# A graph kernel's last stage: VectorE's waits on its own signals become drains, fewer signals per group, another order of its step

## The reference, cut to what matters

```python
h = x @ W
e = jax.nn.leaky_relu((h @ a1)[src] + (h @ a2)[dst], negative_slope=0.2)
attention = jax.nn.softmax(e)                      # over all edges
msgs = attention[:, None] * h[src]
x = _layernorm(x + jax.ops.segment_sum(msgs, dst, num_segments=N))
```

## Time and profile before

| what | us |
|---|---|
| median of three runs | 1265.93 |
| lowest and highest of them | 1257.95, 1266.73 |
| the profiled execution, its own time | 1259.13 |
| its span | 1257.4 |

### The profile page before, as it was taken

How to read it: one execution, slowest core, us unless ns; L and a number is a source line. 1 busy time by engine, 2 the same in 40 slices (tenths; PEclk the granted TensorE clock), 3 DMA queues, 4 the chain that set the end, 5 groups by cost and what they waited for, 6 DMA issues and landing times.

```text
span 1257.4 us, 14313 instructions
## 1 busy us (share of the span) xinstructions
PE 718.7 (57%) x3271; PEld 482.5 (38%) x3271; DVE 759.0 (60%) x3537; ACT 717.2 (57%) x2048; POOL 764.1 (61%) x807
## 2 busy tenths in 40 slices
PE   0357767767667767676844564546455554544441
PEld 0235445445445544444634454545442211111110
DVE  4487767767777668677756555546437444444442
ACT  3457777777777777777713343424347554444443
POOL 7665666666666666665056665666654666666666
PEclk9888888787887888878967777767767766777775
DMA  7365565566665656654155767667755333433331
GB/s 211 110 187 158 184 209 168 178 188 214 203 200 200 203 161 193 197 166 163 68 171 162 216 207 221 198 211 223 208 172 163 121 113 115 119 116 120 107 107 46
DMA packets 89104, 209.87 MB, mean 167 GB/s; under 512 B 20602, under 2 KB 22793, under 8 KB 89008
## 3 DMA queue, kind: packets, MB, share of 16 engines
q1 hardware_dynamic: 63802, 161.20, 40.4%
q0 software_dynamic: 25216, 47.76, 13.6%
HBM read 122.85 MB, written 90.07 MB: 169 GB/s over the span
## 4 chain that ended last, share of the span: by engine, by line
another core or an unknown queue 19%; DVE 17%; ACT 13%; issue 8%; PE 5%; POOL 1%; DMA 1%; DVEq 0%; SPq 0%; POOLq 0%
ACT yb L801 3%; ACT node_out L801 2%; ACT src_b L952 2%; PE psum L748 2%; DVE src_b L1477 2%; DVE match L1152 2%; ACT xsT L961 2%; DVE nst L1492 1%; DVE nst L1254 1%; POOL out_dram L524 1%; DMA x1d_in<-x_all 1%; DVE shift L1485 1%; ACT h_res L965 1%; DVE node_in L1247 1%
## 5 line engine op out<-in xcount | busy, mean ns | idle before, releaser
L518 POOL DMA_INDIRECT xs<-in_x,src_tab x196 | 185.7, 947 | 153.0 <-remote 74.6
L524 POOL DMA_INDIRECT out_dram<-yb,at_last x196 | 194.7, 993 | 120.7 <-ACT yb L801 64.6
L518 POOL DMA_INDIRECT xs<-x_all,row_tab x196 | 187.5, 957 | 114.9 <-issue 55.8
L518 POOL DMA_INDIRECT h_res<-in_x,dst_tab x196 | 188.9, 964 | 59.8 <-issue 59.8
L801 ACT ACTIVATE h_res<-node_in,shift,rstd 128x128 f32<-128x128 f32 (+1 forms) x392 | 155.8, 482 | 0.3 <-DVE shift L1284 0.3
L776 PE MATMUL psum<-src_b,ident_inv 128*128 128x512 f32 x90 | 69.6, 865 | 132.8 <-DVE src_b L1477 111.7
L961 ACT ACTIVATE xsT<-psum 128x512 f32<-128x512 f32 x48 | 28.7, 597 | 200.0 <-remote 165.8
L606 PE MATMUL psum<-h_res 128*128 128x512 f32 x98 | 68.7, 789 | 120.9 <-ACT h_res L808 120.0
L748 PE MATMUL psum<-w,xsT 128*128 128x129 f32 x384 | 80.7, 376 | 91.8 <-ACT xsT L961 80.4
L748 PEld LDWEIGHTS psum<-w,xsT 128*128 128x128 f32 x384 | 71.6, 278 | 99.1 <-ACT xsT L961 86.6
L610 PE MATMUL psum<-xsT,h_res 128*128 128x512 f32 x98 | 85.2, 966 | 32.2 <-ACT xsT L812 19.4
(11 more groups left out here) (312 smaller groups left out, 1915.5 us busy)
## 6 DMA issues: line engine op xcount, KB each, us to landing
x1d_in<-x_all SPq DMA_DIRECT2D x98, 256.0 KB
node_in<-in_x SPq DMA_DIRECT2D x48, 512.0 KB
x_all<-h_res SPq DMA_DIRECT2D x48, 512.0 KB
out_dram<-node_out SPq DMA_DIRECT2D x48, 512.0 KB
x_all<-yb SPq DMA_DIRECT2D x49, 256.0 KB
src_b<-src_t SPq DMA_DIRECT2D x49, 256.0 KB
agg_rows<-src_b SPq DMA_DIRECT2D x49, 256.0 KB
node_in<-x_all SPq DMA_DIRECT2D x24, 512.0 KB
```

Source lines behind the costliest of these rows:

```text
L518: return pool.indirect_dma_start(out=to, out_offset=None, in_=table, in_offset=bass.IndirectOffsetOnAxis(ap=idx, axis=0))
L524: return pool.indirect_dma_start(out=table, out_offset=bass.IndirectOffsetOnAxis(ap=idx, axis=0), in_=rows, in_offset=None, bounds_check=l ...
```

## The change

In the scatters' stage:

- `running(g, t)`: for g > 0 VectorE's wait for its own `r_chain` becomes `dve.drain()`, and its wait for `xa_done` stands before tile 0 alone. Only the last tile of a group signals `r_chain` (all four in group 0), so that a group's sums are complete at `summed(g)` = `G + g`.
- `weigh(g)`: for g > 0 only the last weighed tile of a group signals `xa_done`.
- `moments`: no wait for `e_var`, no signal `e_stats`, one tile per call. `aggregates(b)`: the waits for `e_stats` and `e_shift` go, `dve.drain()` comes.
- ScalarE: between Ln and Exp `act.drain()` in place of the signal `e_log` and its wait.
- VectorE's step s is now: `running(s, 0)`, `shift_of(s - 2)`, `running(s, 1)`, wait for `e_y` of s-1, moments of tile 0, `running(s, 2)`, moments of tile 1, `running(s, 3)`, moments of tiles 2 and 3, `aggregates(s - 1)`.

Ahead of the stage: SyncE waits for the stores of the node rows (`nodes_landed`) before the first three `load_late`; GpSimd waits for the same before stage 2; ScalarE waits for `late_loaded` before it scales late rows.

```diff
+        def summed(g):
+            return G + g
...
+        def nodes_landed(eng):
+            for k in range(GROUPS - NX, GROUPS):
+                eng.wait_ge(x1_stored[k % NX], landed(k, NX))
...
                 if s == GROUPS:
-                    for u in range(NX):
-                        pass
+                    nodes_landed(sp)
                     for j in range(NI):
                         load_late(j)
...
             def weigh(g, tiles=range(G)):
-                wait(act, r_chain, (g - 1) * G)
+                if g >= 2:
+                    act.wait_ge(r_chain, summed(g - 2))
                 for t in tiles:
                     i = g * G + t
-                    fn(tile(xa[:, g % 2, :], t), h_res[:, i * DH:i * DH + D], ACT.Copy, scale=att[:, i:i + 1])\
-                        .then_inc(xa_done, 1)
+                    last = fn(tile(xa[:, g % 2, :], t), h_res[:, i * DH:i * DH + D], ACT.Copy, scale=att[:, i:i + 1])
+                    if g == 0:
+                        last.then_inc(xa_done, 1)
+                if g > 0 and tiles.stop == G:
+                    last.then_inc(xa_done, 1)
...
+                        act.wait_ge(late_loaded[j % NI], use(j, NI) * 16)
...
-                fn(logs[:, 0:G], nmv[:, s % 2, :, 1], ACT.Ln, bias=eps_cols[:, 0:1]).then_inc(e_log, 1)
-                act.wait_ge(e_log, s)
+                fn(logs[:, 0:G], nmv[:, s % 2, :, 1], ACT.Ln, bias=eps_cols[:, 0:1])
+                act.drain()
...
             def running(g, t):
-                dve.wait_ge(xa_done, g * G + (t if g == 0 else G - 1) + 1)
-                wait(dve, r_chain, g * G + t)
+                if g == 0:
+                    dve.wait_ge(xa_done, t + 1)
+                    wait(dve, r_chain, t)
+                else:
+                    if t == 0:
+                        dve.wait_ge(xa_done, summed(g))
+                    dve.drain()
...
-            def moments(b):
-                dve.wait_ge(e_y, b)
-                wait(dve, e_var, b - 1)
-                for t in range(G):
-                    last = v.bn_stats(nst[:, t, :], tile(bank[b % 4], t))
-                last.then_inc(e_stats, 1)
+            def moments(b, t):
+                v.bn_stats(nst[:, t, :], tile(bank[b % 4], t))
 
             def aggregates(b):
-                dve.wait_ge(e_stats, b)
                 if b == 2:
                     dve.wait_ge(first_shift_done, G)
-                wait(dve, e_shift, b - 2)
                 wait(dve, e_rstd, b - 2)
+                dve.drain()
...
                 if edge(s):
-                    for t in range(1, G):
-                        running(s, t)
+                    running(s, 1)
                 if edge(s - 1):
-                    moments(s - 1)
+                    dve.wait_ge(e_y, s - 1)
+                    moments(s - 1, 0)
+                    if edge(s):
+                        running(s, 2)
+                    moments(s - 1, 1)
+                    if edge(s):
+                        running(s, 3)
+                    moments(s - 1, 2)
+                    moments(s - 1, 3)
                     aggregates(s - 1)
```

More of the change, by code:

```diff
@@ L291, in gnn_kernel @@
         agg_stored, part_got = sems("agg_stored", NA), sem("part_got")
-        e_y, e_stats, e_var, e_log, e_rstd, e_shift, e_applied = (
-            sem("e_y"), sem("e_stats"), sem("e_var"), sem("e_log"), sem("e_rstd"), sem("e_shift"), sem("e_applied"))
+        e_y, e_var, e_rstd, e_shift, e_applied = sem("e_y"), sem("e_var"), sem("e_rstd"), sem("e_shift"), sem("e_applied")
         e_scat = sems("e_scat", YB)
@@ L555, in _ @@
             ring_done(pool, x1d_stored, GROUPS, 1)
-            for u in range(NX):
-                pass
+            nodes_landed(pool)
             pool.wait_ge(fix_stored, 16)
@@ L1503, in aggregates, with shift_of @@
                 last.then_inc(e_var, 1)
+            def shift_of(b):
+                dve.wait_ge(e_rstd, b)
+                if b == 2:
+                    dve.wait_ge(first_applied, G)
+                wait(dve, e_applied, b - 2)
+                v.scalar_tensor_tensor(shift[:, b % 2, 0:G], nmv[:, b % 2, :, 0], -1.0, rstd[:, b % 2, 0:G],
+                                       ALU.mult, ALU.mult).then_inc(e_shift, 1)
             def first_rows(t):
@@ L1573, in _ @@
             running(2, 1)
-            moments(1)
+            dve.wait_ge(e_y, 1)
+            for t in range(G):
+                moments(1, t)
             aggregates(1)
```

17 lines of the change are left out of this document (6 added, 11 removed).

## The result

The changed kernel takes 1267.19 us (median of 20 runs, 1261.94 to 1277.01) where the kernel before takes 1260.67 beside it (20 runs, 1253.69 to 1268.45). The ratio is 1.0052, with the interval from 1.003 to 1.0075: half a per cent slower. 1220 was forecast. In the profile the gain isn't lost elsewhere: it never came.

A forecast was written before the change was run, and what follows sets the result against it. GpSimd's scatter issuing, 5.16 us a group with nine holes, was taken to bound the stage. 1259.1 - 41.8 (holes) + 0.5 (waits ahead) = 1217.8, plus 2.3 for the stage's start: 1220 us, range 1208 to 1267.

The forecast's parts named there:

- What bounds the stage: Scatters' stage: GpSimd's issuing, 5.16 us a group, with nine holes of 44.5 us in all from VectorE's late signals.
- The step that failed: VectorE's late own signals: the result was already written, so a drain would not be held; 6.36 us in the cycle shown.
- both gains: VectorE's drains take away lateness between sums, 1.68 + 0.95 us, and from moments to aggregates, 3.73 us, in one cycle.
- 6.36 us of own lateness in a cycle: VectorE's waits for its own signals in the cycle shown, against a GpSimd hole of 4.37 us: enough to close it.
- the sum of 1259.1 - 41.8: Profiled time less GpSimd's nine waits, 44.5 us less 9 times 0.30; with 0.5 added it gave 1217.8 us.
- rival 2: Scatters' stage: something other than engines' signals makes slow steps until GpSimd runs dry; holes stay, 1259 us, chance 0.24.
- Sums and order of the step: VectorE's step: drains between sums taken as 0, at the dearest 0.5 us a step; later sums hidden unless signals are late.
- Signals between engines: `e_var`, `e_shift`, last `r_chain` stay, with 2.2 and 5.1 us lateness; signals fall from 15 to 7 a group, size open.
- The waits ahead of the stage: SyncE's wait for the node store moves loads 0.5 to 3.5 us, taken as 0.5; GpSimd's and ScalarE's new waits 0.
- Rival 1: Lateness moves to the signals that stay, such as `e_var`; half of each hole stays, 1239 us, chance 0.17.
- Rival 3: VectorE's last sum now waits for `e_y` from TensorE; 7.2 us a group in late groups, 1291 us, chance 0.09.
- the one named as decisive: GpSimd's row in the scatters' stage: the prediction is wrong if GpSimd still stands idle every 20 scatters.

The follow-up runs named there:

- few_signals: `few_waits2` with ScalarE signalling `xa_done` only with a group's last tile: 1248.65 us beside 1251.18 for the kernel before, ratio 0.9975.
- more_instr: The kernel before with four one-element writes more in each of VectorE's 48 steps: 1265.76 us against 1258.71, ratio 1.0043.
- few_waits2: The kernel before, all signals kept and no drain, without waits whose condition another wait already covers: 1244.35 us against 1251.18, ratio 0.9961.
- free_scatters: Kernel before, scatters of groups 1 to 47 write a constant tile and wait for nobody: 1041.16 us; `_2`, chip with late completions: 1340.98 beside 1261.81.
- all_oob: Kernel before, groups' scatter bound 0 in place of N - 1, nearly every row skipped: 1041.53 us; `_2`, chip with late completions: 1262.4 beside 1261.81.
- after_old_order: Changed kernel with VectorE's step in the order of before: 1040.01 us against 1040.65, ratio 0.9989; on a second chip 1263.16 against 1258.71, ratio 1.0035.

## Why the prediction was wrong, point by point

**What bounds the stage** was read rightly: GpSimd's issuing at 5.16 us a group with nine holes, made by late completions of VectorE. On the chip with 1040 us the holes are missing, the chain is GpSimd and the stage takes 256.7 us in place of some 300, so the holes were worth fighting.

**The step that failed** is the one on which both gains hang: "only the signal was under way, and a drain, which waits for the engine's own pipeline, would not be held". The prediction counted 6.36 us of own lateness in a cycle as gone. It stayed: 1.55 and 1.56 us at a drain between two sums, and in all 149.6 us of VectorE's idle time in place of 153.6. In the old order 51.6 us stand before the aggregates at the place of 42.4 us of signals. This step came from the instructions' unchanged durations, 0.35, 0.88 and 0.38 us, which are just as unchanged while drains are held, so they say nothing about when an instruction counts as done. The Trainium skill, "Perfetto Trace Analysis", section "Summary: the profiler window per engine type", places the acknowledged write inside the interval; read with that, a drain behind the interval's end should have been free, and here it was not: 1.51 us beyond the end. The measurement decides. With this term gone, the sum of 1259.1 - 41.8 loses its 41.8: the holes came to 46.5 us. The measured 1267.19 lies beside the 1267 at which the range ends, but that is the end kept for rival 2 and says nothing for the mechanism.

**Sums and order of the step.** The fast step was priced at nothing, with 0.5 us as the dear end. From shift to shift it takes 1060.96 - 1057.23 = 3.73 us, with a drain of the first step still held, and 3.52 and 3.53 in the next two, against 3.32: inside the bounds, and covered.

**Signals between engines.** They stayed about as late as they were, 106.0 us at Ln after 107.8, though they had become half as many. "If lateness comes from signals standing in a queue, it shrinks too" was the wrong unit: `few_signals` shows nothing for 144 signals, `more_instr` and `few_waits2` show 0.026 to 0.028 us for each instruction. In that unit the change does nothing in the stage. VectorE has 379 waits before and 94 waits with 240 drains after, ScalarE 48 drains more; all together 3 instructions more. That the unit is the instruction is the best fit of three runs, whose intervals are wide.

**The waits ahead of the stage.** The wait for the node store cost SyncE 2.6 us, inside the 2 to 3.5 estimated. GpSimd's first gather still has `row_tab` as its releaser, after 4.18 us of idle time as in the earlier trace rows, and starts 0.88 us after `row_tab` is made in both kernels, so these 2.6 us were covered there. GpSimd's and ScalarE's waits, put at 0, may not be free as instructions: at the 0.028 us of the scatters' stage, which no run measured ahead of it, 47 of them would be 1.3 us, and 1.0017 and 1.0018 were measured, 2 us. The forecast's 0.5 was too low if that holds.

**The rivals.** Rival 1 gave half of the gain; there was none. Rival 2, nothing changes because something other than the signals makes the slow steps until GpSimd has run dry, had the outcome and the kind of mechanism, at 0.24. The sign that the prediction itself had seen for it, Ln waiting until after the last scatter of 1073.25, was the better evidence, and weighed too little against a reading of what an interval means. Rival 3, sums behind `e_y`, didn't happen: 1.4 us at TensorE in the whole stage, and the old order is as slow as the new. Of the test lines, the one named as decisive was met: GpSimd stands idle every 20 scatters.

**What is left open.** The slowdown of 0.35% to 0.52% is 4.4 to 6.6 us. Some 1.3 to 2 of them can be put to the 47 instructions ahead of the stage, without proof. The rest isn't explained: it isn't the order, and whether a drain costs more than the wait it replaced wasn't measured by itself. Nor do the runs show what the completions share with GpSimd's scatters, or why one chip has none of it. One rival stands untested, the recording of the profile itself, which all these traced executions have in common. The records point at it: the trace of `free_scatters` on the chip without lateness holds 3445 updates of semaphores by engines and 19594 by transfers, that of the same kernel on the chip with lateness 2671 and 5193, so there many are missing. For `all_oob` it is 3440 and 19617 against 2465 and 4531. If recording takes part, some of what was fought here is the price of being profiled.

## What to carry to other kernels

A drain is no way around a late signal: first find out what is late, with a kernel that takes the suspected source away (here the scatters) and one that lets it run free. Where GpSimd issues indirect transfers back to back and completions come late, count instructions on the other engines, waits that stand alone included, and leave out each wait that another covers: here that was worth 0.4%. Compare on one chip only, since the same kernel took 1040 us on one and 1248 to 1262 on the others.

## What the runs showed of the hardware that was not expected

- On a chip with late completions, with scatters issued every 1.29 us almost without a pause, a group of VectorE's work took 18.2 us in place of 3.31 (`free_scatters_2`), though VectorE's instructions kept their durations. Whether the rows of the scatters are written makes no difference (`all_oob_2`: holes of 44.5 us in one run, as before).
- The lateness follows a count: holes are 20 scatters apart in both kernels, and mostly 16 apart with four tiny writes more in a step.
- A drain on VectorE can be held for microseconds after the interval of the last instruction has ended: 1.56 us between sums, and up to 5.8 us ahead of the aggregates.
- Late signals are not bound to scatters. In the first stage of the kernel before (50 to 600 us), where GpSimd gathers, 192 of the 296 signals of TensorE in the trace come over 0.5 us after the end of their matmul, and none of VectorE's 586 or ScalarE's 285. On the chip without lateness it is none of TensorE's 431 (`after_old_order`).
- One chip shows none of this. There the kernel before takes 1040.65 us, and changes to the scatters or to signals move it by 1 us at most. Most of the difference lies ahead of the stage of the change: in `free_scatters`, which is the kernel before up to there, the first scatter starts at 777.3 us there, and at 954.6 in the kernel before on a chip with lateness, 177 us later. In the stage itself it is some 40 us.
